# Sixteen-head attention in two halves of the array's rows, four slots of pairs, additions in batch order

## The reference

```
x += tanh(g_xattn[l]) * attention_l(norm(x), context)      l = 0..3
x += tanh(g_ffn[l])   * feed_forward_l(norm(x))
```

## Time and profile before

| | |
|---|---|
| median of 3 runs | 2148.65 us (2146.74 to 2150.01) |
| the profiled execution | 2144.4 us, span 2142.4 us |
| TensorE, VectorE, ScalarE, GpSimd busy | 78%, 57%, 49%, 33% of the span |
| granted clock of TensorE, mean | 0.853 |
| chain that ended last | TensorE 28%, VectorE, DMA and GpSimd 9% each |

### The profile page before, as it was taken

One profiled execution on the slowest core, in us unless ns is written; L12 is line 12 of the kernel. 1 busy time (PEld: TensorE's weight loads), 2 busy tenths in 40 slices (PEclk: granted clock), 3 DMA queues, 4 the chain that ended last, 5 costly groups with the idle time before them and its releaser, 6 DMA issues.

```text
span 2142.4 us, 42233 instructions
## 1 busy us (share of the span) xinstructions
PE 1678.5 (78%) x14899; PEld 1192.4 (56%) x14902; DVE 1221.5 (57%) x3695; ACT 1054.0 (49%) x2173; POOL 715.9 (33%) x1202
## 2 busy tenths in 40 slices
PE   1778879999958898888999897766657778578434
PEld 0445546767736676664555566655434577467322
DVE  4556655444257667765777664454566642465567
ACT  3445543433326555563555455444334566377456
POOL 5453300200053222213355313252566620621450
PEclk9877889999969889897999999889656799789755
DMA  7555639030025546441222212245554222311100
GB/s 191 123 101 118 127 87 305 23 57 0 1 42 107 108 83 118 88 100 53 52 69 68 58 55 72 71 120 139 161 119 115 68 70 89 89 60 50 43 21 20
DMA packets 189754, 184.44 MB, mean 86 GB/s; under 512 B 29508, under 2 KB 177924, under 8 KB 183556
## 3 DMA queue, kind: packets, MB, share of 16 engines
q1 hardware_dynamic: 180540, 145.04, 29.3%
q10 hardware_dynamic: 816, 19.92, 3.0%
q0 software_dynamic: 8192, 16.79, 2.6%
HBM read 119.47 MB, written 80.74 MB: 93 GB/s over the span
## 4 chain that ended last, share of the span: by engine, by line
PE 28%; DVE 9%; DMA 9%; POOL 9%; issue 7%; ACT 5%; SPq 4%; DVEq 1%; ACTq 0%; POOLq 0%
PE psb L1763 20%; PE psb L1762 4%; DMA Q<-mT 4%; SPq L2808 3%; PE psb L1775 3%; POOL tok_rows L2731 2%; DMA vraw<-in_ctx 2%; POOL KS L2737 2%; DMA K<-tok_rows 1%; POOL K L2737 1%; DVE mneg L2152 1%; DVE X L2349 1%; DVE st L2109 1%; PE psb L1859 1%; ACT HB L2531 0%
## 5 line engine op out<-in xcount | busy, mean ns | idle before, releaser
L2152 DVE TENSOR_REDUCE mneg<-psb 128x4 f32<-128x512 f32 (+1 forms) x576 | 387.6, 684 | 223.3 <-PE psb L1763 220.0
L2531 ACT ACTIVATE HB<-psb 128x512 f32<-128x512 f32 x384 | 222.4, 596 | 186.8 <-PE psb L1763 185.5
L1763 PE MATMUL psb<-Q,K 99*128 99x128 bf16 (+1 forms) x1664 | 250.9, 287 | 75.4 <-DMA Q<-mT 70.2
L1763 PEld LDWEIGHTS psb<-Q,K 99*128 99x128 bf16 (+1 forms) x1664 | 186.3, 136 | 123.4 <-issue 96.1
L1763 PE MATMUL psb<-K,Q 96*128 96x128 bf16 x1280 | 190.3, 252 | 82.3 <-DMA Q<-sc_q 43.7
L2760 POOL TENSOR_SCALAR rs<-mv 128x2 f32<-128x2 f32 (+1 forms) x96 | 21.8, 227 | 622.6 <-DVE mv L2112 613.5
L2531 ACT ACTIVATE HB<-psb,bias 128x512 f32<-128x512 f32 x192 | 131.2, 684 | 166.9 <-PE psb L1763 165.9
L1763 PEld LDWEIGHTS psb<-K,Q 96*128 96x128 bf16 x1280 | 114.4, 112 | 138.5 <-issue 62.0
L1763 PE MATMUL psb<-HB,VA 128*9 128x128 f32 (+1 forms) x2560 | 151.4, 316 | 10.2 <-ACT OE L2536 9.8
L1763 PE MATMUL psb<-KS,Q 96*128 96x128 bf16 x1024 | 148.2, 234 | 11.9 <-DVE mneg L2152 11.5
L1763 PE MATMUL psb<-HB,VS 128*9 128x128 f32 (+1 forms) x2048 | 109.0, 287 | 0.3 <-ACT OE L2536 0.3
(11 more groups left out here) (487 smaller groups left out, 3868.9 us busy)
## 6 DMA issues: line engine op xcount, KB each, us to landing
tok_rows<-in_zero ACTq DMA_DIRECT2D x16, 1152.0 KB, 30.3
K<-sc_k SPq DMA_DIRECT2D x32, 384.0 KB, 5.1
Q<-sc_q SPq DMA_DIRECT2D x32, 384.0 KB
sc_q<-comp SPq DMA_DIRECT2D x48, 192.0 KB, 2.6
K<-tok_rows SPq DMA_DIRECT2D x72, 128.0 KB, 2.1
sc_q<-comp SPq DMA_DIRECT2D x48, 128.0 KB, 2.4
vraw<-in_ctx SPq DMA_DIRECT2D x48, 128.0 KB
KS<-sc_s SPq DMA_DIRECT2D x16, 384.0 KB
```

Source lines behind the costliest of these rows:

```text
L1763: return pe.e.matmul(out, w, x, start=start, stop=stop, skip_group_check=True)
L2152: t = e.tensor_reduce(m.mneg[:, s.b % 4, s.i * A.per:(s.i + 1) * A.per], PSB[s.use.bank].rearrange("p (h k) -> p h k", h=A.per), AX.X, ALU ...
L2531: a.done(act(m.HB[:, s.slot, :], PSB[s.use.bank], ACT.Exp, bias=bz), s.use.drained)
```

## The change

With 16 heads, heads 0 to 7 now stand in rows 0 to 63 and heads 8 to 15 in rows 64 to 127. Each half has its data rows (48; in AF 24 and 24 of zeros), then three rows of maxima in Q8 and ones in K8 and KS. A pair takes 2048 columns, so that four slots fit in the first two thirds of each tile; the third is no longer used for slots. Scores products have 48 rows, weights products 51. A2 keeps 96 and 99 rows. Nothing has to be cleared to zero but the rows that AF leaves empty; ones are set over whole slots. Rows of a pair are loaded by two DMAs in place of one, maxima by two in place of three (A2: one in place of three). The planner's estimates for these steps are changed. `both`, which would issue the products of a scores unit and a weights unit in turn, is there but not used, since `flip` is 0 for all stages. At the end the additions form a chain of their own in batch order, and a group's chain starts when its four additions are done.

```diff
-        "max_rows": lambda: (("pe", 130), ("act", 290), ("sp", 1800)),
+        "max_rows": lambda: (("pe", 130), ("act", 290), ("sp", 650 * A.halves)),
...
-    def place(self, tile, at, H):
-        w = 256 * H
-        return tile[:, at * w // 4096, at * w % 4096:at * w % 4096 + w]
+    def place(self, tile, at):
+        o = 2048 * (at % 2)
+        return tile[:, at // 2, o:o + 2048]
...
-        self.R = 48 // H
+        self.R = 4
+        self.n_rows, self.halves = (96, 1) if dh == 16 else (48, 2)
...
+        self.flip = 0
...
+    def max_rows(self, half):
+        o = 64 * half + self.n_rows
+        return slice(o, o + 3)
...
-            mT_free[k] = ready_m[b] = dma(f"dma_m{k}", 3)
+            mT_free[k] = ready_m[b] = dma(f"dma_m{k}", A.halves)
...
-        do("slot2_clear", need=end)
...
-    may = lambda p, what: 13 + p in st_x1 if what == "loads" else what != "vv" or 12 + p in pv_x1
+    may = lambda p, what: 12 + p in st_x1 if what == "loads" else what != "vv" or 12 + p in pv_x1
...
+    do("k8_ones", i=0, need=E1.begin, done=inc("act", "clear_act"))
...
         for g in range(4 * h, 4 * h + 4):
-            add(lanes[g % len(lanes)], [*[(lambda b=b: add2(b), lambda b=b: got2.get(b, ())) for b in range(4 * g, 4 * g + 4)], *own(g)], 1)
+            first, *others = own(g)
+            add(lanes[g % len(lanes)], [(lambda g=g, f=first: f() if 4 * g + 3 in added2 else False, ()), *others], 1)
+        chain([(lambda b=b: add2(b), lambda b=b: got2.get(b, ())) for b in range(16 * h, 16 * h + 16)], 1)
...
 def heads(tile, p, A, b2, h, rows_, m):
-    o = 256 * h + 128 * b2
-    return m.place(tile, A.at(p), A.H)[0:rows_, o:o + 128]
+    half, at_ = divmod(h, 8)
+    o = 256 * at_ + 128 * b2
+    return m.place(tile, A.at(p))[64 * half:64 * half + A.n_rows + rows_, o:o + 128]
...
-            load(name, dst[0:6 * A.dh, :], sc[p].rearrange("c (d h) t -> (c d) (h t)", d=A.dh))
+            for half in range(2):
+                src = sc[p].rearrange("c (d h) t -> (c d) h t", d=A.dh)[:, 8 * half:8 * half + 8, :]
+                load(name, dst[64 * half:64 * half + 6 * A.dh, :].rearrange("r (h t) -> r h t", h=8), src)
```

More of the change, by code:

```diff
@@ L781, in st_unit @@
             slot = n % A.slots
-            do("weights", A=A, b=b, G=G, kb=kb, use=u, slot=slot, maxima=ready_m[b], free=pt_free[slot], const=t_const, bias=t_biasT)
+            do("weights", A=A, b=b, G=G, kb=kb, use=u, slot=slot, maxima=ready_m[b], free=pt_free[slot], const=t_const, bias=t_biasT,
+               scores=scores)
             if b2 == 1 and i == n_st - 1:
@@ L1793, in scores @@
         out = PSB[s.use.bank]
-        extra = A.bias_i is not None or A.causal
-        pe.wait_ge(s.use.before, s.rows)
         for hh in range(A.per):
@@ L1799, in scores, with score_mask @@
                 o = out[:, 128 * (hh * A.nkb + kb):128 * (hh * A.nkb + kb) + 128]
-                t = matmul(o, heads(m.Q8, p, A, b2, h, 96, m), heads(tiles[kb], p, A, b2, h, 96, m), hh == 0 and kb == 0, not extra, False)
-        if extra:
+                yield matmul(o, heads(m.Q8, p, A, b2, h, 0, m), heads(tiles[kb], p, A, b2, h, 0, m), hh == 0 and kb == 0, s.last, False)
+    def score_mask(s, t):
+        A = s.A
+        o4 = PSB[s.use.bank].rearrange("p (h k) -> p h k", h=4)
+        if not s.last:
             pe.wait_ge(s.bias)
-        o4 = out.rearrange("p (h k) -> p h k", h=4)
         if A.bias_i is not None:
@@ L1809, in scores, with weight_products, weights @@
         pe.done(t, s.use.full)
+    def scores(s):
+        s["last"] = s.A.bias_i is None and not s.A.causal
+        if s.beside:
+            return
+        pe.wait_ge(s.use.before, s.rows)
+        *_, t = score_products(s)
+        score_mask(s, t)
+    def weight_products(s):
+        A, p, b2 = s.A, s.b // 2, s.b % 2
+        tile = ([m.K8] * A.ctx + [m.KS] * A.own)[s.kb]
+        for hh in range(4):
+            h = 4 * s.G + hh
+            yield matmul(PSB[s.use.bank][:, 128 * hh:128 * hh + 128], heads(tile, p, A, b2, h, 3, m), heads(m.Q8, p, A, b2, h, 3, m), hh == 0, not A.causal, False)
+    def weights(s):
+        pe.wait_ge(s.use.before, s.maxima)
+        if s.scores is None:
+            *_, t = weight_products(s)
+        else:
+            pe.wait_ge(s.scores.use.before, s.scores.rows)
+            for t1, t in zip(score_products(s.scores), weight_products(s)):
+                pass
+            score_mask(s.scores, t1)
+        if s.A.causal:
+            pe.wait_ge(s.const)
+            t = matmul(PSB[s.use.bank].rearrange("p (h k) -> p h k", h=4), m.identb[:, :], m.cnegb[:, 1, :].unsqueeze(1).broadcast_to([128, 4, 128]),
+                       False, True, False)
+        pe.done(t, s.use.full)
     def max_rows(s):
@@ L1814, in max_rows @@
         pe.done(pe.e.transpose(PSB[s.use.bank].bitcast(BF16)[0:3 * H, 0:128], m.mcb[:, s.k, 0:3 * H], m.identb[:, :]), s.use.full)
-    def weights(s):
-        A, p, b2 = s.A, s.b // 2, s.b % 2
-        tile = ([m.K8] * A.ctx + [m.KS] * A.own)[s.kb]
-        out = PSB[s.use.bank]
-        pe.wait_ge(s.use.before, s.maxima)
-        for hh in range(4):
-            h = 4 * s.G + hh
-            t = matmul(out[:, 128 * hh:128 * hh + 128], heads(tile, p, A, b2, h, 99, m), heads(m.Q8, p, A, b2, h, 99, m), hh == 0, not A.causal, False)
-        if A.causal:
-            pe.wait_ge(s.const)
-            t = matmul(out.rearrange("p (h k) -> p h k", h=4), m.identb[:, :], m.cnegb[:, 1, :].unsqueeze(1).broadcast_to([128, 4, 128]),
-                       False, True, False)
-        pe.done(t, s.use.full)
     def sums(s):
@@ L2686, in done, with ones @@
         before[0] = g.done(ins, count)
-    def clear(tile, p, ones, count):
+    def ones(tile, at, count):
         g.wait_ge(before[0])
-        if ones:
-            step(e.memset(tile[0:96, p, :], 0.0))
-            g.wait_ge(before[0])
-            done(e.memset(tile[96:128, p, :], 1.0), count)
-        else:
-            done(e.memset(tile[0:96, p, :], 0.0), count)
+        done(e.memset(m.place(tile, at), 1.0), count)
     cleared = [0]
@@ L2710, in ks_clear @@
         g.wait_ge(s.need)
[L2711 removed]
+        ones(m.KS, s.p, count())
     def vs_ones(s):
```

162 lines of the change are left out of this document (87 added, 75 removed).

## The result

The changed kernel takes **2237.5 us** (median; 2221.3 to 2253.2), the kernel before took 2149.3 us beside it. The ratio is 1.038, 95% interval 1.027 to 1.049: **slower**, where I forecast 2132 us and faster. The profiled execution took 2253.2 us, with a span of 2251.3 us. It is the longest of the other three, of which two took 2221.3 and 2221.8 us.

A forecast was written before the change was run, and what follows sets the result against it. TensorE was taken to bound AF and, with holes, A0 and A1; something else A2 and the end. Terms 35 + 31 + 20 - 27 - 33 - 2 - 12 - 3 + 1 - 20 - 6 = -16 us gave 2132 us, range 2085 to 2200.

The forecast's parts named there:

- part 5, the clock: In A0, as TensorE's holes close, the granted clock of 0.82 may rise: -6 us.
- part 1: New changes between 64- and 128-row tiles cost TensorE time: +35 us in AF, +31 in A0, +20 in A1.
- rival B: Half-array tiles load weights slowly, so 16-head products pace at about 0.10 us: about 2320 us; chance 0.06.
- Slots: Four slots issue loads earlier and cut waits: -27 us in A0, -33 in A1; fewer maxima transfers -2 in A2.
- clearing: Memsets between FFN0 and A1 fall away, -12 us; halved KS memsets in A0, -3; extra ones copy at AF, +1.
- rival A: Waits in A0 and A1 only move: SyncE waits for stores, maxima queue behind; 2182 us with 50 of 60 staying; chance 0.27.
- Additions: At the kernel's end, adding in batch order as gathers arrive shortens VectorE's waits: -20 us, bounds 5 and 30.
- Rival C: In the 16-head products, shape changes cost nothing or halves overlap, leaving only gains: 2046 us; chance 0.10.
- Rival D: The kernel's end does not shorten because the last group's chain alone sets it: 2148 to 2152 us; chance 0.12.

The follow-up runs named there:

- whole-array tile: The changed kernel with 16-head products of 96 and 99 rows over the whole array, other edits kept, scores not the reference's: 2051.5 us, ratio 0.958.
- 61 rows against 65: The kernel before with only the rows of 16-head products changed: 61 and 64 rows took 2394.1 us, 65 and 68 rows 2227.7 us.
- the two other traces: The changed kernel with the old order of the last additions (2289.2 and 2292.2 us), and with 61 and 64 rows a half, unit by unit (2220.8 us).

## Why the prediction was wrong

The step that failed is **part 5, the clock**. I took that the holes in A0 close and the granted clock rises, -6 us. It fell: A0 ran wholly at 1.2 GHz, and in the profiled execution so did 181 us at the end of A1 and in AF. By stages that execution against the same kernel with the whole-array tile is +91 us in A0, +48 in A1 and +60 in AF, 199 us; part 1 had 31, 20 and 35, 86 us. Of the 91 us in A0, 27 are the changes of shape (61 rows against 65, both at the lower level), near my 31. The other 64 us are clock. The same subtraction with part 1's own figures leaves 28 in A1 and 25 in AF. The 28 are of that execution alone: in the two other traces A1 is 13 and 14 us above the 306 of the whole-array tile, at the same clock. So the clock cost some 90 us, and in the profiled execution some 115, where I had -6.

The sum then closes on the spans. Part 1 with its clock was 201.5 us (2251.3 against 2049.8) where I had 86, and all the rest gave 92.6 us where I had 102. That turns -16 us into +109, which is 2251.3 against 2142.4; by the medians it is +88.

I had the sign of the clock backwards because I tied it to how full TensorE is. With the whole-array tile that holds (0.81 to 0.89 in A0 from 80 us on). With fewer rows it does not: in A0 of the changed kernel TensorE is busy 243 of 260 us at the lower clock, and before it was busy 212 of 260 us with the full level for more than half of the time.

Part by part:

1. *Shape.* The price was right. I said 0.09 us a change at full clock, from the earlier trace rows; it measured 0.10 to 0.11. At the lower clock I said 0.14 and it was 0.11. The Trainium skill, "TensorEngine Tiling (Array Packing)", Key Properties, says that changing the tiling mode drains the engine; these steps agree. Products kept their pace of 0.055 us at full clock (they start at 850.07, 850.12 and 850.18 us in A1), so rival B was wrong.
2. *Slots* and 3. *clearing.* The sum was near, its parts were not. With the additions they came to 93 us of span where I had 96 (62 + 14 + 20) and 6 for the clock. In A0 I had 27 us off the waits for the maxima, and none went: they are 39.5 us where they were 34.6, and the stage's 15 us came from the clock. That is **rival A**, which I had at 0.27, in the stage and by the path that it named: SyncE stands for GpSimd's split, and the maxima queue behind. In A1 the 33 us came (34.1 to 6.7 and 14.7 to 7.5 us), and 31 us of TensorE's time at a higher clock on top, which no part had: 71 us in all. A2 lost 13 where I had -2. That the sum came out near is luck: the clock in A1 stands in for the waits that stayed in A0. No memset is left between FFN0 and A1, and yet the stretch from A0's last bias to A1's first product stayed at 297 to 300 us, so the 12 us of clearing can only have come later, or not at all.
4. *Additions.* 27 us alone for my 20 (5 to 30): right in kind and nearly in size. In the changed kernel undoing them cost more, 36 to 71 us.

Rival C, that halves overlap, had a true mechanism in the wrong place. In the order of the changed kernel neighbours stay in one half and nothing overlaps. With the order turned, the kernel comes to 2064 us, and with 61 rows to 2031, ahead of my 2046 for C. Rival D was wrong: the end is not set by the last group's own chain alone, as 27 us came off it when that chain began 8 us earlier.

Not shown: why the granted clock follows the rows. Two facts stand. With one tile over the whole array, 65 rows lower it in A0 and 96 rows do not. Two halves side by side with 48 and 51 rows (99 in all) stay low in A0, and with 61 and 64 they do not, though one product of 99 rows was enough in the kernel before. With three slots the 64-row tile lowers it further (0.73 to 0.60 in A1); whether its changes of shape or the idle half do this was not separated. In A1 the rows do not decide alone: the changed kernel holds the full clock there from about 705 us to 938 us, or to the start of AF, and the 61-row kernel with three slots does not. Why was not tried.

## What to carry to other kernels

A matmul over fewer rows costs the same columns and may cost the clock as well: before cutting rows, look for a row at the lower level in the trace, and where rows are free, try to fill them with zeros (61 rows against 48 was worth 33 us here once both halves ran together, and nothing before that). Putting work into half of the array paid here only when the other half's product was issued next to it, in turn, product by product; unit by unit it lost. When a change bundles several edits, price each against the kernel with only that edit: here a gain of 93 us and a loss of 186 us stood in one number. A wait that shrinks is no proof either: A0's wait for the maxima fell to 14.7 us because TensorE was slower. And a stage's time from one trace can be off by 10 us or, where the clock falls at another moment, by 34.

## What the runs showed of the hardware

- In the kernel before, the granted clock fell with the rows that a product uses, while TensorE was busier. All other things equal, 65 rows instead of 96 cost 82 us of 2145 (A0 wholly at the lower level, A1's clock 0.73 for 0.86). In the changed kernel A1 was granted 0.95 with 48 and 61 rows, as with 96.
- A bf16 product of 48 rows paces at 0.055 us for 128 columns, like one of 96. A change between a 64-row and a 128-row tile adds 0.10 to 0.11 us at 2.4 GHz and 0.11 us at 1.2 GHz, but nothing where the number of columns changes at the same place.
- Two products in different halves, issued in turn, run in the time of one (a pair each 0.06 us at full clock, 0.10 at the lower one).
- A stretch with no record of a clock shows as 1.00 in the windows, and raises their means: A0 of the whole-array kernel shows 0.91 in all and 0.89 from its first record on. Only the pace of known matmuls (0.107 us for 128 columns at the lower level, 0.055 at the full one) tells its level.
